# Output stages of a two-attention kernel: where chunks are scaled and split, which engine adds the biases, and the order behind the norm

## Chip, cores and metric

The kernel runs on one core of a Trainium2 chip. Its time is the device time of one execution in microseconds (us); three runs of a kernel are compared by their median. TensorE (PE) multiplies, VectorE (DVE), ScalarE (ACT) and GpSimd (Pool) work on elements, SyncE (SP) issues most of the DMA transfers. Each engine works through its own instructions in order and waits on semaphores for the others.

## What is computed

The input x has 2 sequences of 1024 tokens and 512 features. All matrices are 512 wide, in float32.

```python
x = x + attn_a(layernorm(x)) @ Wo          # 32 heads of 16, latent k and v, rotary positions
x = x + ffn(layernorm(x))                  # x @ W_eff + bias, W_eff = W.T with the LoRA products folded in
x = x + attn_b(layernorm(x)) @ w_proj + b_proj   # q, k, v from w_attn + b_attn; causal, ALiBi
x = x + ffn(layernorm(x))                  # the same ffn again
```

## The kernel before

x stays in SBUF as `x_sb`, 16 tiles of 128 tokens by 512. The work has five parts: projections for attention A (0 to 184 us), attention A (to 885), an output stage called `mid` (to 1182), attention B (to 1653) and an output stage called `fin` (to the end). Each part is one block of instructions for all engines, and the next block begins when all engines are through.

**The attentions** (`run` in `attention_plan`) go through 16 groups of 4 heads, one `step(s)` each. In a step TensorE makes the scores and the value products of group s, and ahead of them the plain scores of the next group for VectorE to take the maxima of (L353, L356). ScalarE takes exponentials (L673) and copies the sums out (L664); SP stores them to DRAM (`oa_sums`, `ob_sums`; the softmax denominators to `za_sums`, `zb_sums`). Pool splits the maxima (L279, L281), and at the end of attention B it also splits two weights into a high and a low part (`to_split`: cast L504, subtraction L506). Attention B works with three slots of memory for the operands of a group, `o_qk`, `second_qk` and `slot_qk`; the last group uses `o_qk`.

**`Output`** brings the sums back by chunks of 512 tokens, of which there are 4 (NC). `load_denominators` and `reciprocals` (L1298) turn the denominators of two chunks around through DRAM; `load(c)` fetches the sums of a chunk (1 MB, L1308) and its reciprocals, broadcast to all rows (4 transfers, L1318); `scale(c)` multiplies the two on VectorE, four instructions of 128x512 (L1324). The sums have two buffers, the broadcast reciprocals one, so `load(c)` waits for `scale(c - 1)` before its last four transfers. In both attentions chunk 0 is loaded in the last step (`s == NG - 1`) and scaled when VectorE is through with the maxima.

**`output_and_ffn`** is both output stages. For step k it makes, in TensorE's order (`order`, written out by hand, also gives each product its PSUM bank, the 8 banks in turn): two tiles of the output product `o` of chunk k, the transposes of the normalised chunk k - 1 (`f_turns`), the other two tiles of `o`, in `mid` also the transposes for the q, k, v projections of chunk k - 2 (`q_turns`), the ffn product `f` of chunk k - 1 (4 tiles), and in `mid` the projections `qk` (8 tiles) and `v` (4 tiles) of chunk k - 2. In `mid` products `o` and `f` are plain float32 (L1505); in `fin` they are made of three products of high and low parts (`split_products`, L806), for which `output_high` (ScalarE, L1576) and `output_low` (VectorE, L1655) split the scaled chunk.

VectorE's order in step k is: the low parts of the transposes (L1649), `scale(k + 1)`, the residual additions of `o` (L1620), with b_proj behind each four in `fin` (L1625), the norm of chunk k (L837 to L850, with Pool's power L855 between), at k = 0 the reciprocals of chunks 2 and 3, `output_low(k + 1)`, in `mid` at k = 0 the split of w_attn (L1682), then the residual of `f` (k - 1) with the ffn bias (L1625) and in `mid` the norm for q. In the last chunk of `mid` TensorE puts maxima of attention B's first groups between its products, in three PSUM banks that both share (`wait_left`).

```python
for k in range(STEPS):
    if fast and 0 <= k - 1 < NC:
        turned_low(f_xnt, k - 1, f_turns[k - 1])
    if k + 1 < NC:
        output.scale(dve, k + 1)
    ...
    if k < NC:
        residual("o", k, out_bias, o_added)
```

Of the kernel before, what the change touches and what calls it, by code (L numbers as in the profile page):

```python
# [1 line left out]

# [12 lines left out]
P = 128  # L15
# [143 lines left out]
def attention_plan(early, nc, ctx, tag, causal, consts, ready, ps_m, rows_of_maxima):  # L159
# [285 lines left out]
    def run(scale, q_d, k_d, v_d, o_d, z_d, alibi_d, ones_d, more, output, late, to_split):  # L445

        with ExitStack() as run_ctx:
# [30 lines left out]
            def _(pool):  # L478
# [24 lines left out]
                for n, (whole, high, low_part) in enumerate(to_split):  # L503
# [3 lines left out]
                                       ALU.subtract).then_inc(w_split, 1)  # L507
                if to_split:
# [3 lines left out]
            def _(sp):  # L512
# [15 lines left out]
                def step(s, j, ahead=True, loads=True):  # L528
# [4 lines left out]
                    if s == NG - 2:  # L533
# [721 lines left out]
class Output:  # L1255
# [6 lines left out]
    def __init__(self, nc, ctx, tag, o_d, z_d, rz_d, o_memory=None, sums=None):  # L1262
# [18 lines left out]
        self.o_scaled = sem("o_scaled")  # L1281

# [45 lines left out]
def output_and_ffn(nc, env, tag, output, w_out, out_bias, nxt, w_eff, early, first=None, second=None):  # L1328
# [28 lines left out]
    with ExitStack() as ctx:  # L1357
# [6 lines left out]
        banks = Banks(nc, ctx, tag, order, early, PT + TPC if nxt else 0)  # L1364
# [4 lines left out]
        if fast:  # L1369

            halves = [slice(n * KC * CHUNK, (n + 1) * KC * CHUNK) for n in range(2)]
            o_parts = [env["first_qk"][:, half].rearrange("p (k t) -> p k t", k=KC) for half in halves]
            o_high_ready = sem("o_high_ready")
            o_split = sem("o_split")
            f_xnt = [env["second_qk"][:, half].rearrange("p (k t) -> p k t", k=KC) for half in halves]
# [3 lines left out]
        added = sem("added")  # L1379
# [20 lines left out]
        o_added, f_added, n = {}, {}, 0  # L1400
        for k in range(STEPS):
            if k < NC and out_bias is not None:
                n += TPC
                o_added[k] = n
            if 0 <= k - 1 < NC:
                n += TPC
                f_added[k - 1] = n

# [7 lines left out]
        def _(sp):  # L1416
            output.load(sp, 1)
# [8 lines left out]
            for k in range(STEPS):  # L1426
# [5 lines left out]
                if not nxt and 0 <= c < NC:  # L1432
                    for t in range(TPC):
                        sp.wait_ge(added, f_added[c] - TPC + t + 1)
# [37 lines left out]
        def _(pe):  # L1472
# [36 lines left out]
            for k in range(STEPS):  # L1509
                def products(tiles):  # L1510
                    natural("o", k, o_parts if fast else [output.o_sb[:, k % 2]], w_out, tiles=tiles)

                if k < NC:

                    pe.wait_ge(o_split if fast else output.o_scaled, KC * (k + 1))
                    products(range(TPC // 2))
                if 0 <= k - 1 < NC:
                    f_norm.transposes(pe, banks, k - 1, f_turns[k - 1], ident)
                if k < NC:
                    products(range(TPC // 2, TPC))  # L1520
# [28 lines left out]
        def _(act):  # L1549
# [20 lines left out]
            def output_high(k):  # L1570
                for kc in range(KC):
                    act.wait_ge(output.o_scaled, KC * k + kc + 1)
                    if k and kc == 0:

                        banks.wait_full(act, ("o", k - 1, TPC - 1))
                    act.activation(o_parts[0][:, kc, :], output.o_sb[:, k % 2, kc, :],  # L1576
                                   ACT.Copy).then_inc(o_high_ready, 1)

            if fast:
                output_high(0)  # L1580
# [288 lines left out]
```

## Time and profile before

| what | value |
|---|---|
| median of 3 runs | 1784.81 us (1781.09 to 1786.96) |
| profiled execution, its own time | 1787.05 us |
| its span, first to last instruction | 1785.2 us |
| mean granted TensorE clock | 0.967 |
| TensorE busy | 1646.3 us, 92% |
| VectorE busy | 1393.8 us, 78% |
| ScalarE busy | 971.8 us, 54% |
| Pool busy | 138.6 us, 8% |

The profile is of one execution. Busy time counts instructions that compute; issuing a transfer or waiting does not count. The granted clock is a share of TensorE's full 2.4 GHz. A row of the timeline gives start, length, engine, line of the kernel, operation and tiles; "x4" is four instructions merged in one row, and in brackets stands how long the engine was idle before it and what released it. "PE" matmuls in `mid` and `fin` have 128 x 512 results; a float32 tile of 512 columns shows as 8 records of L1505, a split tile as 12 of L806.

### The profile page before, as it was taken

How to read it: one execution, taken by the hardware profiler on the slowest of the kernel's cores; microseconds unless marked ns; L12 is line 12 of the kernel's file. 1: busy time of each engine (PE TensorE's matmuls, PEld its weight loads, DVE VectorE, ACT ScalarE, POOL GpSimd, SP SyncE). 2: the span in 40 equal slices, each digit the busy share in tenths (PEclk: the TensorE clock that was granted, in tenths of full speed). 3: DMA queues.
4: the chain of work that ended last, by engine and by line, in shares of the span. 5: the costliest groups of instructions: out<-in, count | busy, mean ns of one | idle time of the engine just before them, and what ended most of it. 6: DMA issues, size and time to landing. Idle time of an engine off the chain costs nothing. (4 is left out here: it accounts for less than half of the span.)

```text
span 1785.2 us, 32918 instructions
## 1 busy us (share of the span) xinstructions
PE 1646.3 (92%) x13040; PEld 849.3 (48%) x13040; DVE 1393.8 (78%) x3007; ACT 971.8 (54%) x1103; POOL 138.6 (8%) x216
## 2 busy tenths in 40 slices
PE   6898999999999999999879999899999999999598
PEld 3554333333333333333335777555454545454476
DVE  3766799999999999999366364568888888885486
ACT  3432277777777777777711112126666666667110
POOL 3332200000000000000000011010000000003000
PEclk9999699999999999999999999989999999999799
DMA  7766334333333332330260433663636363632311
GB/s 217 226 165 193 81 56 85 63 62 64 60 63 65 55 55 56 56 55 12 86 196 1 141 116 104 202 155 57 118 73 103 65 109 60 108 61 63 103 71 71
DMA packets 116801, 167.58 MB, mean 94 GB/s; under 512 B 20772, under 2 KB 58036, under 8 KB 116532
## 3 DMA queue, kind: packets, MB, share of 16 engines
q1 hardware_dynamic: 115176, 160.99, 39.1%
q0 software_dynamic: 1472, 4.49, 1.3%
q8 instruction: 103, 1.69, 0.4%
q14 instruction: 50, 0.41, 0.1%
HBM read 100.41 MB, written 64.50 MB: 92 GB/s over the span
## 5 line engine op out<-in xcount | busy, mean ns | idle before, releaser
L356 DVE TENSOR_REDUCE mxp<-ps_m 128x1 f32<-128x512 f32 x1280 | 799.3, 684 | 69.3 <-PE ps_m L322 63.6
L673 ACT ACTIVATE a_p<-a_ps_s 128x1024 f32<-128x1024 f32 x512 | 522.2, 1025 | 149.8 <-PE a_ps_s L594 138.4
L673 ACT ACTIVATE b_p<-b_ps_s 128x1024 f32<-128x1024 f32 (+1 forms) x320 | 294.7, 938 | 157.9 <-PE b_ps_s L594 154.6
L353 DVE CUSTOM_DVE_ANT_0 ps_m<-ps_m,b_masks 128x128 f32<-128x128 f32 (+3 forms) x512 | 240.1, 517 | 45.1 <-PE ps_m L322 40.9
L322 PE MATMUL ps_m<-slot_qk 62*128 62x512 f32 (+3 forms) x624 | 230.7, 451 | 12.4 <-DVE mxp L356 9.0
L322 PE MATMUL ps_m<-a_slot_qk 62*128 62x512 f32 x640 | 238.1, 450 | 0.8
L594 PE MATMUL a_ps_s<-a_slot_qk 64*128 64x512 f32 x640 | 232.2, 443 | 1.3
L618 PE MATMUL a_ps_o<-a_p,a_slot_v 128*32 128x256 f32 x2560 | 205.6, 390 | 10.0 <-ACT a_p L673 5.4
L594 PEld LDWEIGHTS a_ps_s<-a_slot_qk 64*128 64x128 f32 x640 | 96.2, 185 | 128.8 <-issue 122.7
L594 PE MATMUL a_ps_s<-slot_qk 64*128 64x512 f32 x384 | 136.3, 455 | 0.6
L618 PE MATMUL a_ps_o<-a_p,slot_memory 128*32 128x256 f32 x1536 | 124.3, 393 | 7.4 <-ACT a_p L673 3.3
L322 PEld LDWEIGHTS ps_m<-slot_qk 62*128 62x128 f32 x624 | 101.3, 191 | 39.8 <-DVE mxp L356 27.7
L618 PEld LDWEIGHTS a_ps_o<-a_p,a_slot_v 128*32 128x32 f32 x2560 | 54.9, 108 | 115.1 <-ACT a_p L673 101.5
L574 PE MATMUL b_ps_s<-b_masks 64*128 64x64 bf16 x1024 | 102.1, 197 | 3.0 <-PEq L1357 2.6
L322 PE MATMUL ps_m<-o_qk 62*128 62x512 f32 (+3 forms) x288 | 94.6, 408 | 9.7 <-DVE mid_q_xnt L1649 6.2
L322 PEld LDWEIGHTS ps_m<-a_slot_qk 62*128 62x128 f32 x640 | 99.1, 184 | 9.3 <-DVE mxp L356 8.0
L279 POOL CAST cparts<-negm 128x16 fp32r<-128x16 f32 x64 | 12.6, 197 | 1139.8 <-DVE negm L362 1139.8
L594 PEld LDWEIGHTS a_ps_s<-slot_qk 64*128 64x128 f32 x384 | 56.4, 188 | 78.7 <-issue 74.9
L322 PE MATMUL ps_m<-second_qk 62*128 62x512 f32 (+2 forms) x240 | 87.1, 415 | 3.2 <-DVE mxp L356 1.9
L594 PE MATMUL b_ps_s<-o_qk 64*128 64x512 f32 (+3 forms) x288 | 85.4, 426 | 0.0
L574 PEld LDWEIGHTS b_ps_s<-b_masks 64*128 64x128 bf16 x1024 | 54.8, 96 | 59.0 <-issue 45.1
L1562 ACT ACTIVATE slot_memory<-mid_ps,b_qk 128x512 fp32r<-128x512 f32 x23 | 15.8, 689 | 109.0 <-PE mid_ps L806 92.8
(205 smaller groups left out, 2343.7 us busy)
## 6 DMA issues: line engine op xcount, KB each, us to landing
va_groups<-w_o SPq DMA_DIRECT2D x16, 512.0 KB, 3.7
ka_parts<-pa_parts SPq DMA_DIRECT2D x16, 512.0 KB, 3.8
qa_parts<-pa_parts SPq DMA_DIRECT2D x32, 256.0 KB, 3.7
kb_parts<-slot_memory SPq DMA_DIRECT2D x16, 512.0 KB, 4.1
qb_parts<-slot_memory SPq DMA_DIRECT2D x32, 256.0 KB, 3.8
vb_groups<-w_proj SPq DMA_DIRECT2D x16, 512.0 KB, 3.4
a_slot_qk<-qa_parts SPq DMA_DIRECT2D x60, 128.0 KB, 4.1
a_slot_qk<-ka_parts SPq DMA_DIRECT2D x48, 128.0 KB, 6.3
```

Source lines behind the costliest of these rows:

```text
L279: pool.tensor_copy(cparts[:, :, 0, :], split(negm[:, :])).then_inc(high_ready, 1)
L322: pe.matmul(ps_m[:, bank_of(g, i), 0:keys], q, k, start=True, stop=True).then_inc(piece_ready, 1)
L353: dve.tensor_tensor_reduce(from_, from_, mask_of_query[:, CHUNK - keys:], 1.0, LOWEST, ALU.add, ALU.max, accum_out=to).then_inc(piece_take ...
L356: dve.tensor_reduce(to, from_, AX.X, ALU.max).then_inc(piece_taken, 1)
L574: pe.matmul(to[:, half * ROW_TILE:(half + 1) * ROW_TILE], mask[tile, half, :], half_ident[tile, :], start=(half == 0), stop=False, skip_gr ...
L594: mm = pe.matmul(to[:, at:at + n], k, q, start=not diagonal, stop=True, skip_group_check=diagonal)
L618: mm = pe.matmul(ps_o[VW * h:VW * (h + 1), off:off + n], slots[j].v[:, kt, VW * h:VW * (h + 1)], p_sb[:, (2 * u + h // 2) % NP, h % 2, at: ...
L673: act.activation(p_sb[:, (2 * u + pair) % NP, :, off:CHUNK], ps_s[:, 2 * pair:2 * pair + 2, off:CHUNK], ACT.Exp, scale=scale).then_inc(exp ...
L1562: act.activation(parts[:, n % PARTS, 0, :], banks.out(("qk", c, i)), ACT.Identity, bias=bias_of(i)).then_inc(high_ready, 1)
```

## The change

- **Chunks 0 and 1 in the attentions' last groups.** Denominators, reciprocals and loads of the first batch move one step earlier (`NG - 3`, `NG - 2`), and `load(1)` is new in the last step. At the end of VectorE's list stand `scale(0)` and `scale(1)`. In attention B both are split there as well, high parts by Pool (`high_pool`) and low parts by VectorE (`low`), into two buffers of parts in `second_qk` and `slot_qk`, which groups 13 and 14 have left. In `fin` the transposed chunk moves to `o_qk`.
- **Biases by Pool.** b_proj is added to x by Pool in attention B, one tile behind each part of the maxima (`to_add`), before the output stage. The ffn bias is added by Pool behind the norm of the tile it belongs to (`biased`), before the residual of `f`. VectorE's L1625 is gone.
- **Scaling behind the norm.** `scale(k + 1)` and, in `fin`, its split come after the norm of chunk k, for chunks 2 and 3 only. `reciprocals(1)` comes first in the stage. The split of w_attn moves from k = 0 to k = 1.
- **Transposes behind 3 products**: three tiles of `o`, the transposes, the fourth tile, in TensorE's order and in the banks. VectorE takes the residuals of the first three tiles, the low parts of the transposes, then the fourth residual.
- In `mid` the last 16 tasks (with the last q transposes) use the five own banks, before it was the last 12.

```diff
@@ run of attention_plan
+                adds = iter(to_add)
                 for g in range(1, NG):
                     for qh in range(2):
                         parts_of_maxima(g, qh)
+                        for tile, bias in itertools.islice(adds, 1):
+                            pool.tensor_tensor(tile, tile, bias, ALU.add)
...
+                if output.split:
+                    for c in range(2):
+                        pool.wait_ge(pv_done, (NG - 2 + c) * NU)
+                        output.high_pool(pool, c)
...
-                    if s == NG - 2:
+                    if s == NG - 3:
                         for qh in range(2):
                             sp.wait_ge(out_stored[qh], output.STORES * s)
                         output.load_denominators(sp, 0)
-                    if s == NG - 1:
+                    if s == NG - 2:
                         output.store_reciprocals(sp, 0)
                         output.load(sp, 0)
+                    if s == NG - 1:
+                        output.load(sp, 1)
...
-                    if s == NG - 2:
+                    if s == NG - 3:
                         output.reciprocals(dve, 0)
-                output.scale(dve, 0)
+                for c in range(2):
+                    output.scale(dve, c)
+                    if output.split:
+                        output.low(dve, c)
@@ class Output
+    def high_pool(self, pool, c):
+        for kc in range(KC):
+            pool.wait_ge(self.o_scaled, KC * c + kc + 1)
+            pool.tensor_copy(self.parts[c % 2][0][:, kc, :], self.o_sb[:, c % 2, kc, :]).then_inc(self.high_ready, 1)
...
+    def low(self, dve, c):
+        for kc in range(KC):
+            dve.wait_ge(self.high_ready, KC * c + kc + 1)
+            dve.tensor_tensor(self.parts[c % 2][1][:, kc, :], self.o_sb[:, c % 2, kc, :],
+                              self.parts[c % 2][0][:, kc, :].bitcast(F32), ALU.subtract).then_inc(self.split_ready, 1)
@@ output_and_ffn
-            order += [("o", k, t) for t in range(TPC // 2)]
+            order += [("o", k, t) for t in range(TPC - 1)]
         if 0 <= k - 1 < NC:
             order += f_turns[k - 1]
         if k < NC:
-            order += [("o", k, t) for t in range(TPC // 2, TPC)]
+            order += [("o", k, TPC - 1)]
...
-        banks = Banks(nc, ctx, tag, order, early, PT + TPC if nxt else 0)
+        banks = Banks(nc, ctx, tag, order, early, KC + PT + TPC if nxt else 0)
...
-            output.load(sp, 1)
...
-                if fast and k + 1 < NC:
-                    output_high(k + 1)
+                if fast and 2 <= k + 1 < NC:
+
+                    banks.wait_full(act, ("o", k - 1, TPC - 1))
+                    output.high_act(act, k + 1)
...
                     f_norm.gpsimd(pool, k)
+                    for t in range(TPC):
+                        tile = x_sb[:, k * TPC + t, :]
+                        pool.wait_ge(f_norm.xn_ready, k * TPC + t + 1)
+                        pool.tensor_tensor(tile, tile, w["bias"][:, :], ALU.add).then_inc(biased, 1)
...
+            output.reciprocals(dve, 1)
             for k in range(STEPS):
-                if fast and 0 <= k - 1 < NC:
-                    turned_low(f_xnt, k - 1, f_turns[k - 1])
-                if k + 1 < NC:
-                    output.scale(dve, k + 1)
                 if nxt and k == 2:
                     dve.wait_ge(ones_set, 1)
                 if k < NC:
-                    residual("o", k, out_bias, o_added)
+                    residual("o", k, range(TPC - 1))
+                if fast and 0 <= k - 1 < NC:
+                    turned_low(f_xnt, k - 1, f_turns[k - 1])
+                if k < NC:
+                    residual("o", k, [TPC - 1])
                 if nxt and 0 <= k - 2 < NC:
                     turned_low(q_xnt, k - 2, q_turns[k - 2])
                 if k < NC:
                     f_norm.vector(dve, k, k, k and (lambda: banks.wait_full(dve, f_turns[k - 1][-1])))
...
-                if nxt and k == 0:
+                if 2 <= k + 1 < NC:
+                    output.scale(dve, k + 1)
+                    if fast:
+                        output.low(dve, k + 1)
+                c = k - 1
+                if 0 <= c < NC:
+                    residual("f", c)
+                    if nxt:
+                        q_norm.vector(dve, c, c, c and (lambda: banks.wait_full(dve, q_turns[c - 1][-1])))
+                if nxt and k == 1:
                     for kc in range(KC):
                         dve.wait_ge(w_high_ready, kc + 1)
```

## Rows read from the trace of the kernel before

**Rows 1.** Windows by stage: length; busy (instructions) PE, PEld, DVE, ACT, POOL; clock, DMA, GB/s
```profile
884.90:1182.00 297.10, 277.30 (x1012) 175.88 (x1012) 162.00 (x319) 44.07 (x69) 17.62 (x15) 0.97 0.44 132
1182.00:1653.00 471.00, 444.89 (x4876) 236.01 (x4876) 395.84 (x1266) 312.21 (x352) 33.64 (x74) 0.98 0.46 84
1653.00:1785.20 132.20, 102.74 (x448) 83.44 (x448) 86.95 (x162) 17.04 (x32) 4.05 (x4) 0.89 0.24 83
```

**Rows 2.** Waits, 1650 to 1786 us: us in total, times, longest
```profile
PE fin_ps L806 <- DVE o_qk L1655: 22.1, 4, 13.3
...
PE fin_ps L806 <- DVE second_qk L1649: 2.3, 1, 2.3
```

**Rows 3.** Timeline, first output stage: start, length, instruction, [idle before <- releaser]
```profile
914.67 5.02 DVE L1682 TENSOR_TENSOR mid_w_qkv<-slot_memory,mid_w_qkv 128x1536 fp32r<-128x1536 f32 x3
...
926.89 2.50 DVE L1324 TENSOR_TENSOR o_memory<-o_memory,out_a_rzt 128x512 f32<-128x512 f32 x4 [5.52 <-DMA out_a_rzt<-za_reciprocals]
...
930.04 5.49 PE L1505 MATMUL mid_ps<-w_eff,ffn_memory 128*128 128x512 f32 x8 [8.39 <-DVE x_sb L1620]
...
935.37 10.46 PE L1505 MATMUL ps_m<-w_eff,ffn_memory 128*128 128x512 f32 x24
```

**Rows 4.** Timeline, end of the first output stage
```profile
1127.88 0.69 DVE L1641 TENSOR_TENSOR w_proj<-ps_m,b_v 128x512 f32<-128x512 f32 x1 [9.47 <-DMA vb_groups<-w_proj]
...
1130.00 2.47 DVE L1649 TENSOR_TENSOR mid_q_xnt<-mid_ps,mid_q_xnt 128x512 fp32r<-128x512 f32 x4
...
1131.04 0.47 PE L322 MATMUL ps_m<-o_qk 62*128 62x128 f32 x2 [6.24 <-DVE mid_q_xnt L1649]
```

**Rows 5.** Chain of waits in order of time, one chunk of the last stage
```profile
1705.04 2.47 DVE fin_f_stats L837 x4
...
1709.11 1.92 DVE fin_f_xn L850 x4
...
1711.04 2.42 DVE o_qk L1655 x4
```

**Rows 6.** Timeline of Pool and VectorE, projections at the start
```profile
62.17 2.70 POOL L1174 TENSOR_TENSOR o_memory<-o_memory,pa_cos 128x512 f32<-128x512 f32 x2
...
62.24 3.83 DVE L850 TENSOR_SCALAR ffn_memory<-x_sb,pa_mv,pa_rstd 128x512 f32<-128x512 f32 x4 [1.12 <-POOL pa_rstd L855]
...
72.58 0.69 DVE L1204 TENSOR_TENSOR w_q<-pa_ps,pa_sin 128x512 f32<-128x512 f32 x1 [1.81 <-PE pa_ps L1040]
...
73.12 1.27 POOL L1174 TENSOR_TENSOR o_memory<-w_proj,pa_cos 128x512 f32<-128x512 f32 x1
...
73.31 1.63 DVE L1208 TENSOR_TENSOR w_q<-o_memory,w_q 128x512 f32<-128x512 f32 x1
```

**Rows 7.** End of attention B: Pool's groups of 1629.5 to 1652.4 us, then timeline
```profile
L506 POOL TENSOR_TENSOR w_proj_low<-w_proj,w_proj_high 128x2048 fp32r<-128x2048 f32 x1 | 4.6, 4554 | 0.1
...
L504 POOL CAST w_proj_high<-w_proj 128x2048 fp32r<-128x2048 f32 x1 | 1.9, 1891 | 0.0
...
1635.90 2.54 SPq L1318 DMA_DIRECT2D out_b_rzt<-zb_reciprocals  x4
...
1646.56 2.50 DVE L1324 TENSOR_TENSOR out_b_o_t<-out_b_o_t,out_b_rzt 128x512 f32<-128x512 f32 x4 [15.69 <-DMA out_b_rzt<-zb_reciprocals]
...
1653.56 1.83 SPq L525 DMA_DIRECT2D ob_sums<-out_b_sums  x4
```

**Rows 8.** Windows of products in the last stage, and its last transposes from the timeline
```profile
1659.00:1664.40 5.40, 5.38 (x13) 4.28 (x14) 0.00 (x0) 0.00 (x0) 0.00 (x0) 0.53 0.73 230
1664.40:1672.60 8.20, 8.20 (x36) 6.41 (x35) 4.30 (x7) 0.00 (x0) 0.00 (x0) 1.00 0.18 56
1766.60:1771.10 4.50, 4.46 (x13) 3.59 (x14) 1.69 (x3) 0.00 (x0) 0.00 (x0) 0.63 0.22 84
...
1762.47 1.91 PE L865 MATMUL fin_ps<-ident,fin_f_xn 128*128 128x128 f32 x16
```

**Rows 9.** Timeline, VectorE's last instructions
```profile
1780.06 2.49 DVE L1625 TENSOR_TENSOR x_sb<-x_sb,b_ffn 128x512 f32<-128x512 f32 x4
```

More of the change, by code:

```diff
@@ L443, in attention_plan, with run @@
     early.tensor, early.vector, early.banks = early_tensor, early_vector, ps_m
-    def run(scale, q_d, k_d, v_d, o_d, z_d, alibi_d, ones_d, more, output, late, to_split):
+    def run(scale, q_d, k_d, v_d, o_d, z_d, alibi_d, ones_d, more, output, late, to_split, to_add):
         with ExitStack() as run_ctx:
@@ L1281, in __init__ @@
         self.o_scaled = sem("o_scaled")
+        self.split = parts_memory is not None
+        if self.split:
+            self.parts = [[m[:, n * KC * CHUNK:(n + 1) * KC * CHUNK].rearrange("p (k t) -> p k t", k=KC)
+                           for n in range(2)] for m in parts_memory]
+            self.high_ready = sem("o_high_ready")
+            self.split_ready = sem("o_split")
     STORES = 16 * (GH + 1)
@@ L1510, in products @@
                 def products(tiles):
-                    natural("o", k, o_parts if fast else [output.o_sb[:, k % 2]], w_out, tiles=tiles)
+                    natural("o", k, output.parts[k % 2] if fast else [output.o_sb[:, k % 2]], w_out, tiles=tiles)
                 if k < NC:
-                    pe.wait_ge(o_split if fast else output.o_scaled, KC * (k + 1))
-                    products(range(TPC // 2))
+                    pe.wait_ge(output.split_ready if fast else output.o_scaled, KC * (k + 1))
+                    products(range(TPC - 1))
                 if 0 <= k - 1 < NC:
@@ L1569, in _ @@
                     act.activation(w_qkv[0][:, kc, :], w_whole[kc], ACT.Copy).then_inc(w_high_ready, 1)
[L1570 to L1580, printed above, removed]
             for k in range(STEPS):
@@ L1615, in _, with residual @@
         def _(dve):
-            def residual(kind, c, bias, counts):
-                for t in range(TPC):
+            def residual(kind, c, tiles=range(TPC)):
+                for t in tiles:
                     task, tile = (kind, c, t), x_sb[:, c * TPC + t, :]
                     banks.wait_full(dve, task)
+                    if kind == "f":
+                        dve.wait_ge(biased, c * TPC + t + 1)
                     dve.tensor_tensor(tile, banks.out(task), tile, ALU.add).then_inc(banks.drain(task), 1)
-                for t in range(TPC):
-                    task, tile = (kind, c, t), x_sb[:, c * TPC + t, :]
-                    banks.wait_drained(dve, task)
-                    if bias is not None:
-                        dve.tensor_tensor(tile, tile, bias[:, :], ALU.add).then_inc(added, 1)
-                if bias is not None:
-                    dve.wait_ge(added, counts[c])
+                for t in tiles:
+                    banks.wait_drained(dve, (kind, c, t))
             def low(c, i):
@@ L1683, in _ @@
                                           ALU.subtract).then_inc(w_split, 1)
-                c = k - 1
-                if 0 <= c < NC:
-                    residual("f", c, w["bias"], f_added)
-                    if nxt:
-                        q_norm.vector(dve, c, c, c and (lambda: banks.wait_full(dve, q_turns[c - 1][-1])))
                 c = k - 2
@@ L1804, in build @@
                         [(env["w"]["proj"][:, :, :], env["w_proj"].rearrange("(k p) n -> p k n", p=P))],
-                        [(env["w"][name], *split[name]) for name in ("proj", "eff")])
-            output_and_ffn(nc, env, "fin", output, split["proj"], env["w"]["bproj"], False, split["eff"], early_b)
+                        [(env["w"][name], *split[name]) for name in ("proj", "eff")],
+                        [(env["x_sb"][:, n, :], env["w"]["bproj"][:, :]) for n in range(TILES)])
+            output_and_ffn(nc, env, "fin", output, split["proj"], False, split["eff"], early_b)
 def in_parts(x):
```

47 lines of the change are left out of this document (16 added, 31 removed).

## Prediction

> **What bounds the kernel now.** I read first the windows by stage [rows 1]. TensorE is busy 277.3 of 297.1 us in the first output stage and 102.7 of 132.2 us in the last one, where its granted clock is 0.89 against 0.97 and 0.98. In the attentions it is above 94%. So idle TensorE is to be had in the two output stages and hardly elsewhere: 19.8 and 29.5 us, and some more where the clock is low.
>
> Then the waits, and what ended each. In the last stage four waits of 22.1 us together (longest 13.3) are for the low parts of the attention output [rows 2]. In the first output stage TensorE stood 8.4 us for a residual addition of VectorE [rows 3] and 6.2 us for VectorE's low parts of the last q transposes [rows 4]. The timeline says what was late behind the 8.4 us [rows 3]: VectorE sat 5.52 us in `scale(2)`, which waits for the broadcast reciprocals; the residuals that free the PSUM banks are queued behind it. After the wait a product tile takes 5.49 us, where three later ones take 10.46. For the 6.2 us [rows 4]: VectorE stood 9.47 us because the stores of v came late. In SP's order they stand behind the stores of this chunk's k and q and the loads of the next attention's first group, so this end hangs on when VectorE gives SP its first piece, and four bias additions (2.49 us, as in [rows 9]) lie ahead of that. In the last stage the chain of waits runs through VectorE and Pool from one chunk to the next [rows 5].
>
> **First output stage, step by step.** The profiled execution took 1787.05 us, its span is 1785.2, the median of the runs is 1784.81; I sum against the span and carry the difference over.
> - Chunk 1 is loaded and scaled inside attention A, whose VectorE is idle after its last maxima. o(0) runs as now, and o(1) follows with no wait.
> - Three product tiles of o(1) (10.5 us by the three of f in [rows 3]) go ahead of the transposes, so these wait for no norm. f(0) finds its banks drained, since the residuals are no longer behind `scale(2)`: the 8.4 us wait goes, and 2.0 us of low clock behind it (5.49 against 10.46 / 3 = 3.49).
> - The split of w_attn (three of its four instructions took 5.02 us [rows 3], so 6.7 of VectorE) moves to k = 1, behind it Pool's memset of 128x2048 (I take 1.9, as the Pool cast of that size in [rows 7]) and then the residuals of o(2), on which the first q transposes wait: by my schedule about 0.5 us lost; f(0)'s 14 us and three tiles of o(2) cover the rest. Sum to the first q product: 8.4 + 2.0 - 0.5 = 9.9.
> - The end: the last f tile sets VectorE; without the biases its first piece comes 2.5 us earlier, SP's row of DMAs with it, and the 6.2 us wait shrinks by that. The q transposes of the last chunk now use the five banks that are not shared with the maxima, so the first maxima needn't wait for them: 0.7 us (of the 1.0 from 1130.00 to 1131.04, [rows 4]). Stage: 9.9 + 2.5 + 0.7 = 13.1 us gained.
>
> **The price: Pool's bias additions beside VectorE.** Four additions of 128x512 a chunk now start as each normalised tile is ready, while VectorE still normalises the next. Rows of the first stage show what the two do to each other [rows 6]: with two Pool tensor_tensors beside them, four normalisations took 3.83 us instead of 1.92 [rows 5], 0.95 us for each Pool instruction; a VectorE tensor_tensor with both inputs in SBUF took 1.63 instead of 0.69, also 0.94 more; one that reads PSUM and SBUF took 0.69, untouched. The engines take turns. So two additions fall between the normalisations (+1.9) and the other two between the four multiplications of `scale`, where one follows (+1.9); residuals are not touched. Bounds: 0 (VectorE keeps ahead), and 4 x 1.27 = 5.1 if each holds VectorE for its length. I take 3.8, the measured delay. The Trainium skill, page SBUF — State Buffer, section "SBUF: two separate sides", says the pair shared by VectorE and GpSimd is an exclusive lock, and the loser "fully blocks", also for a VectorE operation with two SBUF inputs. The trace agrees in kind; by its letter the sum would be the upper bound, 5.1 a chunk. In the first output stage 3.8 us a chunk stay hidden: o(1) covers chunk 0, f(0) of 14 us covers chunk 1; without that cover each would cost its 3.8.
>
> **End of attention B.** `scale(0)`, with two SBUF inputs, now starts at about 1630.4, beside Pool's two casts and two subtractions of the weights (1.89 and 4.55 us each, [rows 7]). Taking turns, its four instructions end at about 1643.5 instead of 1632.8. SP issues the reciprocals of chunk 1 only then. Now they and the 1 MB of outputs land 10.7 us after the first issue (1635.90 to 1646.56); without the 1 MB I take 8.5, so 1652. Scale, Pool's casts and the low parts by turns: 5.6, to 1657.6. SP's last DMA of the block used to set its end, 1655.4 [rows 7]; now VectorE does, and the stage begins at 1658.0. Bounds: 1655.9 (no turns), 1660.5 (10.7 us again). SP also holds the store of group 15's first half behind this wait, without cost, as the second half's store comes later still.
>
> **Last output stage.** A product tile takes 2.73 us, the first one after a pause 5.4 at a granted clock of 0.53, about the lower level of 1.2 GHz [rows 8]; the transposes of a chunk take 1.8 (1.91 to the end of the last [rows 8]). From the stage's start: o(0) 5.4 + 8.2 = 13.6. Chunk 1 is split already: three tiles, 21.8; transposes, which wait 0.4 for the fourth normalised tile, 24.0; fourth tile 26.7. From there VectorE's way to o(2): residual 0.6, norm to its last tile 6.0 (1705.04 to 1711.03), low parts 2.4 [rows 5], scale 2.4 (four instructions of the same size, 2.50 with the last one's end [rows 3]), and 3.8 for Pool: 15.3 with rounding. f(0), 11.0 us, covers it except 4.3, and after such a pause the clock is low again (1.8 more for the tile after a wait of 2.3 us [rows 2, 8], 2.6 after a longer one; I take 2.3). o(2) starts at 42.0; three tiles 52.5, transposes 54.3, fourth 57.0. The same once more: o(3) starts at 72.3, its fourth tile ends at 87.3. Chunk 3 has no successor: f(2) to 98.3, transposes 100.1, f(3) 111.1. Residual 0.7. The last additions of b_ffn (2.49, [rows 9]) are gone, also those of b_proj (2.5 a chunk, done by Pool in attention B); from VectorE's last instruction (1782.55) to the end of the span 2.7 as now. Total 114.5; 1658.0 + 114.5 = 1772.5, which is 12.7 us before 1785.2.
>
> **Attentions.** The reciprocals of batch 0 (1.8 us of VectorE) move one group earlier. In A there is a like place now. In B they fall where VectorE is busy nearly all of a group (395.8 of 471.0 us over the whole attention, its last group idle [rows 1]), and delay maxima on which TensorE waits: up to 1.8. The 16 additions of b_proj run beside VectorE instructions that read PSUM and at most one SBUF operand, the untouched kind: 0, at most 16 x 0.94 = 15. The moved DMAs (two denominators, two reciprocals, one load of five) cost SP some 5 us in a group of about 29 (471.0 / 16), well before the next load it owes. I take 1.5 us lost in all.
>
> **Sum.** 13.1 + 12.7 - 1.5 = 24.3 us: span 1760.9, profiled 1762.8, and against the median of 1784.81, 1760.5 us.
>
> **Rivals.**
> - No price for Pool: VectorE keeps ahead and nothing takes turns. The stage begins at 1655.9; both stalls shrink from 4.3 to 0.5 us and cost no clock: 2.1 + 2 x (3.8 + 2.3) + 0.4 = 14.7 more. 1745.8 us. For it: Pool's first addition can only start after the second normalisation is under way. Against: the turns in [rows 6].
> - Dearer: each addition blocks for its length, the reciprocals are late (+2.5), the stalls grow by 1.3 each, the first stage gets a stall and low clock (3), the attentions lose 2 more: 10 us back, 1770. For it: at the end of attention B VectorE, Pool and SP now work one behind the other. Against: the 0.94 us of [rows 6]. It is also where the Trainium skill's rule of the exclusive lock (page and section as above) leads.
> - The maxima of attention B do collide with b_proj's additions: 15 us back, 1775. The untouched instruction in [rows 6] speaks against it.
> - Slower: the pauses of 4.3 us leave TensorE's clock at its low level through the rest of the last stage. Then 20 tiles from o(2) on take 5.4 instead of 2.73 and the kernel ends 29 us later than now, at 1813 (24.3 gained, 53 lost). It decides from 9 tiles at the low level. Against: after the pause ahead of the stage's first product and the one of 2.3 us the clock was full, or all but, one tile later [rows 8].
> - The change doesn't do what it says: chunk 1 ready only after the stage's start. That needs the block's end past VectorE, which it waits for; then the start is late instead, as priced.
>
> **Chances.** As summed 0.52; no price 0.19; dearer 0.18; collision in B 0.04; lost to within 0.3% (5.4 us, what a measurement here can tell from no change) by several of these 0.03; slower 0.04. So faster 0.93, same 0.03, slower 0.04. The range goes from just below the no-price case to just above the dearer one: 1744 to 1772.
>
> **What would show it.** No wait ahead of the first f product and first q product some 10 us earlier; normalisation rows of 3.8 us a chunk with Pool additions of 1.3 to 1.7 between; in attention B's end `scale(0)` stretched over some 13 us and the last stage starting near 1658; there two TensorE waits of about 4 us before o(2) and o(3), none of 13; no addition after the last residual. Wrong if the normalisations take 1.9 or if the waits before o(2) and o(3) pass 7 us.

## The result, and the profile after

The changed kernel takes 1765.03 us (median of 4 runs, 1764.1 to 1765.98) against 1784.47 us for the kernel before (4 runs, 1781.09 to 1786.96): ratio 0.9892, 95% interval 0.9875 to 0.991. The forecast was 1760.5 us in a range of 1744 to 1772. The profiled execution took 1764.37 us with a span of 1762.2 (before 1787.05 and 1785.2).

I cut both traces at the same four places: first o product of the first output stage (`mid`), first score product of attention B, last value product of B, first o product of the last stage (`fin`). Each part is the difference of two rows of TensorE's timeline:

| part | before | after | gained | forecast |
|---|---|---|---|---|
| start to `mid` | 887.93 | 886.86 | 1.07 | 0 |
| `mid` | 295.99 | 282.48 | 13.51 | 13.1 |
| attention B to its last product | 468.38 | 469.21 | -0.83 | -1.5 |
| from there to `fin` | 6.72 | 7.21 | -0.49 | 1.0 |
| `fin` to the end of the span | 126.18 | 116.44 | 9.74 | 11.7 |

The windows by stage after answer to [rows 1]; the last three lie behind TensorE's restarts at 1687.75 (5.5 and 7.25 us) and 1719.40 (5.5 us), ahead of o(2) and o(3):
```profile
886.80:1169.30 282.50, 274.43 (x1012) 175.02 (x1012) 160.58 (x299) 44.27 (x68) 40.79 (x31) 0.98 0.44 133
1169.30:1638.60 469.30, 445.05 (x4876) 235.83 (x4876) 410.84 (x1270) 311.88 (x351) 58.06 (x94) 0.98 0.48 87
1645.70:1762.20 116.50, 103.09 (x448) 83.75 (x448) 73.55 (x118) 13.19 (x24) 27.56 (x20) 0.92 0.21 75
...
1687.70:1693.20 5.50, 5.45 (x13) 4.31 (x14) 2.38 (x4) 0.00 (x0) 0.00 (x0) 0.50 0.77 259
1687.75:1695.00 7.25, 7.25 (x20) 5.75 (x21) 3.02 (x5) 0.00 (x0) 0.00 (x0) 0.59 0.71 245
1719.40:1724.90 5.50, 5.50 (x14) 4.36 (x15) 2.35 (x5) 0.00 (x0) 0.00 (x0) 0.54 0.51 191
```
TensorE's idle time in `mid` fell from 19.8 to 8.1 us, in `fin` from 29.5 to 13.4. Its waits in `fin`, which answer to [rows 2]:
```profile
PE fin_ps L822 <- PEq L449: 7.2, 1, 7.2
PE fin_ps L822 <- DVE second_qk L1369: 4.8, 1, 4.8
PE fin_ps L822 <- DVE slot_qk L1369: 4.8, 1, 4.8
PE ps_m L881 <- DVE fin_f_xn L866: 0.3, 1, 0.3
```
In place of four waits of 22.1 us there are two of 4.8, ahead of o(2) and o(3). Behind each, TensorE ran at the lower of its two clock levels, 1.2 GHz instead of 2.4. The first 7.25 us from the first restart had a granted clock of 0.59, which is 7.25 x 0.41 = 3.0 us lost; behind the second it is 5.5 x 0.46 = 2.5 us. VectorE's way to o(2), its timeline (answers to [rows 5]):
```profile
1676.81 3.88 DVE L866 TENSOR_SCALAR fin_f_xn<-x_sb,fin_f_mv,fin_f_rstd 128x512 f32<-128x512 f32 x4 [1.13 <-POOL fin_f_rstd L871]
1680.61 4.67 DVE L1348 TENSOR_TENSOR out_b_o_t<-out_b_o_t,out_b_rzt 128x512 f32<-128x512 f32 x4
1685.21 2.48 DVE L1369 TENSOR_TENSOR second_qk<-out_b_o_t,second_qk 128x512 fp32r<-128x512 f32 x4
```
and Pool beside it:
```profile
1677.43 6.09 POOL L1627 TENSOR_TENSOR x_sb<-x_sb,b_ffn 128x512 f32<-128x512 f32 x4 [0.66 <-DVE fin_f_xn L866]
```
Pool's additions lie under the normalisation and the scaling, and both are stretched; the low parts behind them are not. Within the four scalings only two are stretched, and the first stands alone in a narrower view:
```profile
1680.61 1.78 DVE L1348 TENSOR_TENSOR out_b_o_t<-out_b_o_t,out_b_rzt 128x512 f32<-128x512 f32 x1
```
At the end of attention B (answers to [rows 7]), VectorE and then SP:
```profile
1616.64 13.87 DVE L1348 TENSOR_TENSOR out_b_o_t<-out_b_o_t,out_b_rzt 128x512 f32<-128x512 f32 x4
1631.02 3.70 DVE L1369 TENSOR_TENSOR second_qk<-out_b_o_t,second_qk 128x512 fp32r<-128x512 f32 x4 [0.50 <-POOL second_qk L1356]
1638.88 3.32 DVE L1348 TENSOR_TENSOR out_b_o_t<-out_b_o_t,out_b_rzt 128x512 f32<-128x512 f32 x4 [4.17 <-DMA out_b_rzt<-zb_reciprocals]
1642.13 3.31 DVE L1369 TENSOR_TENSOR slot_qk<-out_b_o_t,slot_qk 128x512 fp32r<-128x512 f32 x4
```
```profile
1630.60 2.55 SPq L1342 DMA_DIRECT2D out_b_rzt<-zb_reciprocals  x4
...
1639.82 1.83 SPq L536 DMA_DIRECT2D ob_sums<-out_b_sums  x4
```
`scale(0)` lasts 13.87 us beside Pool's split of the weights; SP asks for chunk 1's reciprocals when it ends; VectorE's work ends last (1642.13 + 3.31 = 1645.44), behind the issue of SP's last store. In `mid` the 8.4 us wait is gone, one of 1.9 stands ahead of the first q transposes, and the wait of 6.2 us at the end ([rows 4]) is 2.7:
```profile
PE ps_m L324 <- issue: 2.7, 1, 2.7
...
PE mid_ps L881 <- DVE x_sb L1649: 1.9, 1, 1.9
```

### The profile page after: what moved, and what is told of

It reads as the page before. It is cut to its first block and busy times, and to the rows that moved or that the text cites. A ratio compares the mean times of both kernels' runs of the same rounds, so it can differ in the third digit from the quotient of the medians.

```text
span 1762.2 us, 32974 instructions
## 1 busy us (share of the span) xinstructions
PE 1643.6 (93%) x13040; PEld 848.8 (48%) x13040; DVE 1402.5 (80%) x2959; ACT 969.0 (55%) x1095; POOL 213.8 (12%) x272
## 5 line engine op out<-in xcount | busy, mean ns | idle before, releaser
L324 PE MATMUL ps_m<-slot_qk 62*128 62x512 f32 (+3 forms) x624 | 230.9, 451 | 12.2 <-DVE mxp L358 8.9
```

The source lines that it names most:

```text
L324: pe.matmul(ps_m[:, bank_of(g, i), 0:keys], q, k, start=True, stop=True).then_inc(piece_ready, 1)
```

## The experiments

The theory was that Pool's additions of b_ffn, where they stand, cost the two waits and the clock behind them, and that Pool's split of the weights makes `fin` start late. The rival was that VectorE's chain or SP sets both anyway. All edits are against the changed kernel. The parts are by the same cuts, from each profile. Only `fin` is cut short here, at the end of its last product in a bank of `fin_ps`; three more tiles, 8.2 us in every kernel, follow it.

| kernel | `mid` | B | gap | `fin` | span | median |
|---|---|---|---|---|---|---|
| before | 295.99 | 468.38 | 6.72 | 112.15 | 1785.2 | 1784.47 |
| after | 282.48 | 469.21 | 7.21 | 105.02 | 1762.2 | 1765.03 |
| v1_pool_late | 281.39 | 470.11 | 6.59 | 91.04 | 1744.5 | 1751.65 |
| v2_split_early | 282.57 | 478.47 | 3.54 | 103.50 | 1760.9 | 1763.01 |
| v3_bias_vector | 288.15 | 472.95 | 6.99 | 93.62 | 1762.1 | 1764.98 |
| v4_two_products | 286.61 | 472.56 | 7.97 | 109.44 | 1772.5 | one run |
| v5_chunk1_in_stage | 283.90 | 472.73 | 3.53 | 113.05 | 1768.4 | one run |
| v6_both | 280.77 | 470.24 | 3.53 | 90.82 | 1740.5 | 1746.47 |
| v7_halves | 281.81 | 472.27 | 6.89 | 103.54 | 1760.7 | one run |
| v8_both_apart | 281.74 | 467.95 | 3.53 | 92.17 | 1741.5 | 1743.67 |
| v9_banks | 284.44 | 472.79 | 7.70 | 103.11 | 1765.2 | one run |
| v10_scale_first | 284.56 | 474.98 | 7.11 | 103.39 | 1765.5 | one run |
| v11_wsplit_first | 286.85 | 468.27 | 7.39 | 105.23 | 1764.9 | one run |
| v12_all | 281.40 | 469.25 | 3.53 | 91.63 | 1742.5 | 1743.18 |

The start of `mid`, behind code that is nearly the same in all, varies from 881.5 to 887.9 us; so spans of single runs are compared part by part. A part varies as well. `mid` is the same code in the changed kernel, v2 and v5: 282.5, 282.6 and 283.9 us. `fin` is the same in the changed kernel, v2, v9, v10 and v11: 105.0, 103.5, 103.1, 103.4 and 105.2 us. In `fin` the waits are the same too (4.8 us twice); what differs is how long the clock stays low behind them. A difference of 2 us in a part, seen in one profile, is therefore not resolved by the time alone.

**v1_pool_late.**
```diff
+                    pool.wait_ge(f_norm.xn_ready, (k + 1) * TPC)
+                    if 2 <= k + 1 < NC:
+                        pool.wait_ge(output.split_ready if fast else output.o_scaled, KC * (k + 2))
                     for t in range(TPC):
                         tile = x_sb[:, k * TPC + t, :]
-                        pool.wait_ge(f_norm.xn_ready, k * TPC + t + 1)
                         pool.tensor_tensor(tile, tile, w["bias"][:, :], ALU.add).then_inc(biased, 1)
```


> Pool adds b_ffn only when VectorE has normalised the chunk and scaled (in the last stage also split) the next one, so no addition lies beside a VectorE instruction with two SBUF inputs. Theory (the two engines take turns on such instructions, and that alone makes the two waits of 4.8 us): four normalisations 1.9 instead of 3.87 us, four multiplications 2.4 instead of 4.67; the two waits of TensorE fall to 0.6 us each, the low clock behind them (about 2.7 us each) goes; last stage 116.4 to about 103 us, span 1762.2 to about 1748.5, median about 1751. Rival 1 (the waits come from VectorE's chain itself, or the residuals of f now wait for the late additions): the last stage stays within 2 us of 116.4, 1763 to 1767. Rival 2 (the waits go but the clock is low anyway): two times 4.2 us, median about 1757.

VectorE's timeline of the same chunk, and then Pool's:
```profile
1672.57 1.92 DVE L866 TENSOR_SCALAR fin_f_xn<-x_sb,fin_f_mv,fin_f_rstd 128x512 f32<-128x512 f32 x4 [1.13 <-POOL fin_f_rstd L871]
1674.40 2.49 DVE L1348 TENSOR_TENSOR out_b_o_t<-out_b_o_t,out_b_rzt 128x512 f32<-128x512 f32 x4
```
```profile
1679.45 5.06 POOL L1629 TENSOR_TENSOR x_sb<-x_sb,b_ffn 128x512 f32<-128x512 f32 x4 [6.92 <-DVE second_qk L1369]
```
Waits of TensorE and the window of `fin`:
```profile
PE fin_ps L822 <- DVE second_qk L1369: 0.6, 1, 0.6
PE fin_ps L822 <- DVE slot_qk L1369: 0.6, 1, 0.6
```
```profile
1642.00:1744.50 102.50, 97.69 (x448) 79.93 (x448) 61.57 (x118) 13.02 (x24) 24.30 (x20) 0.98 0.24 85
```
Both waits are 0.6 us, the clock is 0.98, `fin` is 14.0 us shorter: 8.4 of waits, 5.5 of clock, 0.1 elsewhere. Median 1751.65 us, ratio to before 0.9825 (0.980 to 0.9849). The profiled execution was the fastest of the four (1746.69); by the medians the gain is 13.4 us. The theory holds (`fin` with its end 102.4 us, 103 expected); both rivals fell.

**v2_split_early.** Pool's split is cut by kc and done one piece behind each part of the maxima from group 9 on.
```diff
-                for n, (whole, high, low_part) in enumerate(to_split):
-                    pool.tensor_copy(high[:, :, :], whole[:, :, :]).then_inc(w_high_ready, 1)
...
+                pieces = iter([(*t, kc) for t in to_split for kc in range(KC)])
...
                         parts_of_maxima(g, qh)
+                        for whole, high, low_part, kc in itertools.islice(pieces, 1 if g >= 9 else 0):
...
+                            pool.tensor_copy(high[:, kc, :], whole[:, kc, :]).then_inc(w_high_ready, 1)
...
```


> The split of w_proj and w_eff on Pool is cut into pieces of 128x512 and moved from the end of attention B into its groups 9 to 12. Theory (the late start of the last stage comes from scale(0) of chunk 0 being stretched by Pool's casts and subtractions to 12.3 us, behind which SP's load of the reciprocals waits): scale(0) takes 2.5 us, the last VectorE instruction of the block ends about 3.7 us earlier, the gap from the last PV product to the stage's start falls from 7.2 to 3.5 us; span 1762.2 to about 1758.5, median about 1761.5. Rival (the gap is set by SP's last stores, or by the loads themselves): gap stays above 6 us, median 1764 to 1766. A loss is possible if the pieces delay Pool's small work on the maxima in groups 9 to 12: it would show as TensorE waits inside attention B.

VectorE's timeline, and windows of 5 us in group 14:
```profile
1620.54 2.48 DVE L1352 TENSOR_TENSOR out_b_o_t<-out_b_o_t,out_b_rzt 128x512 f32<-128x512 f32 x4
...
1636.56 3.33 DVE L1352 TENSOR_TENSOR out_b_o_t<-out_b_o_t,out_b_rzt 128x512 f32<-128x512 f32 x4 [9.34 <-DMA out_b_rzt<-zb_reciprocals]
```
```profile
1584.00:1589.00 5.00, 3.86 (x48) 2.16 (x48) 4.82 (x18) 2.40 (x4) 0.42 (x2) 1.00 0.07 17
1589.00:1594.00 5.00, 5.00 (x43) 2.38 (x40) 2.92 (x12) 2.54 (x3) 0.00 (x0) 0.54 0.47 122
1594.00:1599.00 5.00, 5.00 (x37) 3.22 (x35) 2.88 (x11) 1.80 (x3) 0.00 (x0) 0.50 0.68 252
```
The end went as the theory says: `scale(0)` 2.48 us, gap 3.54. But B took 9.3 us more. Its windows show two stretches at half clock, this one and one from about 1238, behind a wait of 1.72 us for the shift rows. v6_both, with the same split, has neither (470.24 us), so the split is not their cause. Median 1763.01, ratio 0.9875 (0.9854 to 0.9895): its gain alone is not resolved from the changed kernel.

**v3_bias_vector.** Pool's four additions go; VectorE adds b_ffn behind the residuals of f, and SP's store waits for that.
```diff
                 for t in tiles:
                     banks.wait_drained(dve, (kind, c, t))
+                    if kind == "f":
...
+                        dve.tensor_tensor(tile, tile, w["bias"][:, :], ALU.add).then_inc(biased, 1)
```


> b_ffn is added by VectorE again, behind the residual of each f product, in both output stages; b_proj stays with Pool in attention B. Theory (the price of the moved additions is their turns with VectorE): normalisations 1.9, multiplications 2.4 us, both waits of 4.8 us fall to 0.6 and their low clock goes (about -14), but four additions (2.5 us) are back behind the last residual of each stage, so +2.5 at the end and +2.5 at the end of the first output stage: span about 1753, median about 1756. Rival (the moved additions are worth what they were moved for): VectorE becomes the bound again, its 2.5 us a chunk bring the waits back, median 1765 or more.

`fin` to its last product is 11.4 us shorter, and the four additions are back behind it:
```profile
1756.93 2.49 DVE L1648 TENSOR_TENSOR x_sb<-x_sb,b_ffn 128x512 f32<-128x512 f32 x4
```
The two waits are 0.6 us again, so in `fin` the theory of the turns holds here too. But a wait that I had not counted, 2.26 us ahead of f(3), stands for low parts behind VectorE's additions:
```profile
1745.05 0.47 PE L822 MATMUL fin_ps<-w_eff_high,o_qk 128*128 128x512 f32 x1 [2.26 <-DVE o_qk L1672]
```
With the four additions at the end, `fin` as a whole is 8.8 us shorter. What I had more wrong is `mid`, 5.7 us longer where I expected 2.5:
```profile
PE ps_m L324 <- DVE w_proj L1664: 6.0, 1, 6.0
...
PE mid_ps L881 <- DVE x_sb L1643: 3.0, 1, 3.0
```
against 2.7 and 1.9 in the changed kernel. The median, 1764.98 us, is that of the changed kernel, as the rival had it (1765 or more), though not by the rival's waits. In the two profiles b_ffn on Pool gains 5.7 us in `mid` and loses 8.8 in `fin`; what evens this out is B, 3.7 us longer here, with a stretch at half clock that the changed kernel's profile lacks (see the last section).

**v4_two_products.** `TPC - 1` back to `TPC // 2` in the order, the banks, TensorE's and VectorE's lists.

> Transposes of the normalised chunk again behind two of the four o products, the rest as changed. Theory (the fourth normalised tile is ready just as the third product ends): the transposes of f wait for the normalisation by a product's time less what is hidden, in the last stage 2.3 us for chunk 0 and nothing for chunks 1 and 2, whose transposes come long after the norm; in the first output stage the residuals on which f's banks hang come earlier in VectorE's row. Together +2 to +5 us, span 1764 to 1767. Rival (the order of products is indifferent): span within 1 us of 1762.2.

`mid` is 4.1 and `fin` 4.4 us longer, more than I expected. Two of the waits for the norm of chunk 0 in `fin`, of which I had counted 2.3 us together and no clock:
```profile
1672.22 0.33 PE L881 MATMUL ps_m<-ident,fin_f_xn 128*128 128x128 f32 x1 [1.08 <-DVE fin_f_xn L866]
1673.63 1.33 PE L881 MATMUL ps_m<-ident,fin_f_xn 128*128 128x128 f32 x5 [1.08 <-DVE fin_f_xn L866]
```
In this profile the order is worth 8.5 us. The waits make up about half: TensorE waits 1.8 us more in `fin` and 1.9 more in `mid`. The clock is the other half: summed over slices of 1 us, (1 - granted clock) x length is 10.9 us instead of 8.7 in `fin` and 6.8 instead of 4.7 in `mid`. A new low stretch stands right behind the second of the two waits shown.

**v5_chunk1_in_stage.** Chunk 1 of B is loaded, scaled and split (high parts by ScalarE) ahead of the loop of `fin`.
```diff
-                    for c in range(2):
+                    for c in range(1):
                         pool.wait_ge(pv_done, (NG - 2 + c) * NU)
                         output.high_pool(pool, c)
...
+            if fast:
+                output.scale(dve, 1)
+                output.low(dve, 1)
             output.reciprocals(dve, 1)
```


> Chunk 1 of attention B is loaded, scaled and split in the last output stage instead of in the attention's last group, the rest as changed. Theory (the late start, 7.2 us behind the last product of the attention, is the price of doing chunk 1 there; in the stage its 8.5 us of load lie beside o(0) of 14 us): the gap falls to about 3.6 us, chunk 1 is split about 15 us into the stage, TensorE waits up to 2 us ahead of o(1); last stage to its last product 105 to 108 us; sum within 3 us of the changed kernel. Rival (doing chunk 1 early is what removed the old waits): a wait of over 5 us ahead of o(1), sum 5 us or more worse.

```profile
1661.36 0.50 PE L822 MATMUL fin_ps<-w_proj_high,slot_qk 128*128 128x512 f32 x1 [3.94 <-DVE slot_qk L1369]
```
The gap is 3.53 us as expected, but the reciprocals landed 12.5 us after the stage's start, not 8.5, and o(1) waited 3.94 us. `fin` is 8.0 us longer: chunk 1 in attention B is worth 8.0 - 3.7 = 4.3 us. That lies between the theory (within 3) and the rival (5 or more); the wait, 3.94 us, does too.

**v7_halves.** Each addition of 128x512 as two of 128x256.

> Each of Pool's additions of b_ffn (128x512) is cut into two of 128x256: the same work in twice as many instructions. If each turn costs VectorE the rest of one Pool instruction, halving them lowers the price: normalisations below 3.87 us, nearer to 2.9, multiplications below 4.67. If what counts is the bandwidth of shared work (both engines slowed in proportion), the two stay at 3.9 and 4.7 us. Last stage 112 to 116.5 us by the one, 116 to 118 by the other.

```profile
1676.95 2.76 DVE L866 TENSOR_SCALAR fin_f_xn<-x_sb,fin_f_mv,fin_f_rstd 128x512 f32<-128x512 f32 x4 [1.13 <-POOL fin_f_rstd L871]
1679.63 4.66 DVE L1348 TENSOR_TENSOR out_b_o_t<-out_b_o_t,out_b_rzt 128x512 f32<-128x512 f32 x4
1684.21 3.54 DVE L1369 TENSOR_TENSOR second_qk<-out_b_o_t,second_qk 128x512 fp32r<-128x512 f32 x4
```
Neither theory as written. The three together take 10.96 us, 11.03 in the changed kernel, and 6.90 in v1_pool_late: the price is 4.1 us either way. Halves take half the turn each (normalisation 2.76 instead of 3.88), but there are twice as many: all four scalings are stretched (4.66 in sum, as before), and the rest lands on the low parts (3.54 instead of 2.48). `fin`, 103.54 us, is no shorter than with whole additions (103.1 to 105.2).

**v10_scale_first.** In `mid` alone, `scale(k + 1)` stands ahead of the residuals of o(k) again.

> In the first output stage alone, VectorE scales chunk k + 1 ahead of the residuals of o(k) again; chunk 1 is still scaled in attention A, all else as changed. Theory (the old wait of 8.4 us came from the residuals being queued behind scale(2), which waits for the broadcast reciprocals; moving the scaling behind the norm took it away, not the early chunk 1): TensorE waits again ahead of the first f product, 5 to 9 us, with a low clock behind it; stage 282.5 to 289 to 294 us. Rival (early chunk 1, with its earlier loads, is what took it away): scale(2) finds its reciprocals landed and the stage stays within 2 us of 282.5.

```profile
910.44 2.72 DVE L1348 TENSOR_TENSOR o_memory<-o_memory,out_a_rzt 128x512 f32<-128x512 f32 x4 [1.99 <-DMA out_a_rzt<-za_reciprocals]
```
My theory fell: `mid` is 2.1 us longer (1.2 of it a longer wait ahead of the first q transposes, 3.1 instead of 1.9) and no wait stands ahead of f(0). `scale(2)` begins 26.4 us into the stage (910.44 - 884.03), 39.0 before (926.89 - 887.93). The reciprocals come 12.5 us earlier, and with them in time the place of the scaling matters little. The reverse, the new order with late reciprocals, was not run.

**v9_banks.** `KC + PT + TPC` back to `PT + TPC`.

> The transposes of the last q chunk use all eight PSUM banks again instead of the five that are not shared with the first maxima of attention B. Theory: the wait of TensorE behind the last q transposes' drain is 0.7 us longer, stage 283.2 instead of 282.5. Rival (the end of the stage hangs on the loads of the first group alone): no change, 282.5 within 0.5.

The wait at the end of `mid` is 3.65 us for the low parts of the transposes instead of 2.68: 1.0, where I had 0.7. The stage is 2.0 longer; the other 1.0 is clock, 5.7 us lost in the stage instead of 4.7 by the same sum over slices. This half is scatter: v5, with `mid` unchanged, has the longer low stretch at the same place and takes 283.9 us.

**v11_wsplit_first.** `if nxt and k == 1` back to `k == 0` for the split of w_attn, ahead of the scaling.

> VectorE splits w_attn at k = 0, behind the norm of chunk 0, instead of at k = 1. Theory (the 1.94 us wait of TensorE ahead of the first q transposes comes from the split and Pool's memset behind it, both ahead of the residuals of o(2)): the wait falls to 0.7 us or less and the stage is 1 to 2 us shorter, 280.5 to 281.5, if f(0) finds its banks. Rival (the split at k = 0 delays the residuals of o(1) and so f(0), which it was moved for): a wait of 2 to 5 us ahead of the first f product, stage 284 or more.

```profile
920.60 4.97 PE L1537 MATMUL mid_ps<-w_eff,ffn_memory 128*128 128x512 f32 x7 [2.78 <-DVE x_sb L1649]
```
The rival held: the wait ahead of the q transposes goes, one of 2.78 us ahead of f(0) comes, and the stage is 4.4 us longer.

**v6_both, v8_both_apart, v12_all**: v1 and v2 together; with the two reciprocals of group 13 apart; with v11's edit as well.

> Late additions of b_ffn and early split of the weights together. Theory (independent places): last stage to its last product 91 us as with the late additions alone, gap ahead of it 3.5 us as with the early split alone, first output stage 281.4; attention B 469 to 478 us, depending on how often a short wait of TensorE in it is followed by a low clock. Span 1736 to 1748, likeliest 1741, median about 1744. Rival (the early split itself costs attention B some 9 us, as it seemed in its own run): B again 478 us and median about 1750, no better than the late additions alone.

> As the run with both, and the two reciprocals that VectorE computes back to back behind the maxima of group 13 in attention B stand apart: one in the middle of that group's maxima, one at the end. Theory (1.8 us of VectorE in one piece let TensorE wait 0.97 us for its maxima there, and after that wait the clock was low for about 10 us in three of five kernels, some 4 to 5 us each time): the wait falls to 0.3 us or less, no low clock near group 14, B at most 470 us; median 2 to 4 us below the run with both. Rival (the wait is not the cause of the low clock, or z's load comes too late for the middle of the group, so that VectorE stands there): a low stretch at the same place, or a new wait of TensorE inside group 13; the same time or more.

> The run with both and the reciprocals apart, and the split of w_attn at k = 0 as well. Theory: first output stage 280 instead of 281.7, the rest as there: median 1742, 1739 to 1745. Rival: the split at k = 0 costs more than it gives back, median 1745 to 1750.

v6 is v1's `fin` and v2's gap, as expected: median 1746.47 us, ratio 0.979 (0.977 to 0.981). v8: 1743.67, 0.9781 (0.9756 to 0.9807); its wait did not fall to 0.3 us but moved, 0.9 us in group 13. v12: 1743.18, 0.978 (0.9763 to 0.9798). The three are not told apart by time; each beats both kernels. In v12, where Pool's additions no longer slow VectorE, the early split of w_attn costs nothing, but it gains less than the 1.7 us I expected over v8 (281.40 against 281.74).

## Why the prediction was right

- **`mid`, 13.1 forecast, 13.5 measured.** Up to the first q product 9.9 us were gained (976.23 - 887.93 = 88.3 before, 965.29 - 886.86 = 78.4 after), as forecast, and 3.6 at the end, 3.2 forecast. The sum is right and its terms less so. The wait of 8.4 us went, but I gave one cause, the residuals standing behind `scale(2)`. v10_scale_first shows that the new order was not needed: with the old order back, reciprocals that land 12.5 us earlier keep the wait away. Whether the order alone would have done it too is open. The change held both, so the term came out by luck as much as by reading. The earlier landing may be due to `reciprocals(1)` standing first or to `load(1)` having left the stage; this was not tried apart, but SP's rows speak for the first. It stores the reciprocals right behind VectorE's, 26.0 us into the stage before and 4.4 after (a row of before, then one of after):
```profile
913.97 1.14 SPq L1303 DMA_DIRECT2D za_reciprocals<-out_a_z  x2
...
891.23 0.99 SPq L1327 DMA_DIRECT2D za_reciprocals<-out_a_z  x2
```
  The q transposes wait 1.94 us, not 0.5, for residuals of o(2) that stand behind Pool's memset, as VectorE's timeline says:
```profile
949.08 1.89 DVE L1649 TENSOR_TENSOR x_sb<-mid_ps,x_sb 128x512 f32<-128x512 f32 x3 [1.90 <-POOL w_proj L1621]
```
  What makes up for it lies ahead of f(0), where o(0), the first transposes and o(1) take 2.1 us less, a gain that I had put at nothing; behind f(0) some 0.6 us are lost again.
- **The price of Pool's additions** was the term to get right, and its kind and size hold: 4 x 0.95 = 3.8 us a chunk forecast, 4.1 measured (11.03 - 6.90). The term was small by 0.3, in `scale` (4.67 against 2.49): two normalisations lost 0.98 us each (3.88 - 1.92), as forecast, but two scalings 1.09 each ((4.67 - 2.49) / 2), where I had taken 0.95 for all. One scaling takes 1.78 us beside Pool and 0.68 in v1_pool_late, while beside the residuals, with one input in PSUM, Pool's additions stay at 1.27 us each (5.06 for four). Pool is held up by the turns too: beside the SBUF-only instructions its four take 6.09 us. The Trainium skill, page SBUF — State Buffer, section "SBUF: two separate sides", calls the shared pair an exclusive lock whose loser is fully blocked; the runs agree in kind, but in size four additions of 5.06 us cost VectorE 4.1, not 5.1.
- **The two waits**: 4.8 us instead of 4.3, by that 0.3 and rounding; low clock 3.0 and 2.5 instead of 2.3 each. v1_pool_late shows the chain from cause to time: additions moved, waits and low clock gone, 14.0 us. The rival "no price" put the two waits and their clock at 2 x 6.1 = 12.2. The clock's share is not fixed: in v2, v9 and v10 the same two waits of 4.8 us cost 1.5 to 1.7 us of clock each, and `fin` is 1.5 to 1.9 us shorter for it.
- **The late start**: 7.2 us behind the last value product against 5.7 forecast. `scale(0)` ended 13.9 us after its start, 13.1 forecast; the reciprocals landed 8.3 us after their first issue (8.5 forecast); the mis-sized term is scale and split of chunk 1, 6.6 us instead of 5.6, because Pool's casts stretch both. v2_split_early shows the cause. The gap it leaves, 3.5 us, is the least in any kernel here, and `mid` too begins 3.5 us behind attention A in all of them.
- **Attentions**: 1.5 us forecast, 0.8 measured. No wait of TensorE in B's profile is put down to Pool's additions of b_proj, as forecast. But the moved reciprocals left a wait that I had priced at nothing more than its length (below).
- **The sum**: the span came out 1.3 us above the 1760.9 forecast. That it came so near is partly luck: the two terms of `fin` and its late start fell short by 3.5 us, and 1.1 of that was made good by a `mid` that began earlier, which is within that start's scatter, 0.7 by B and 0.4 by `mid`. The other 3.2 us between 1760.5 and 1765.0 are the step from one profiled execution to the median: before, the profiled execution lay 2.2 us above the median (1787.05, 1784.81), after, 0.7 below it (1764.37, 1765.03), and its ends took 2.2 us instead of 1.9.

The changed kernel's largest remaining fault is where it adds b_ffn: v3_bias_vector gives the same median with the additions back on VectorE, and v1_pool_late 13.4 us less with them later on Pool.

## What to carry to other kernels

In this kernel Pool's additions were free beside VectorE's residuals, which read PSUM; next to instructions with SBUF inputs alone they cost VectorE 4.1 us for 5.06 us of their own, some four fifths, whole or in halves. Put such work behind the last such instruction of the chain that TensorE waits for: the same additions, behind the scaling and the low parts, gave 14.0 us in `fin` and 13.4 by the medians. And when a wait disappears, test which of the moved things removed it: here an earlier DMA was enough without the new order.

## What the runs showed of the hardware

A wait of TensorE of under 1 us can cost several. Moving two reciprocals to the end of group 13 made TensorE wait 0.95 to 0.98 us in group 14, in eleven of the kernels above. In seven of them the granted clock then stood at about half for some 10 us (0.54 and 0.50 in the rows of v2_split_early), in four it stayed at 1.00, as in the changed kernel:
```profile
1584.00:1589.00 5.00, 3.86 (x51) 2.38 (x43) 4.82 (x19) 2.36 (x4) 0.42 (x2) 1.00 0.09 21
1589.00:1594.00 5.00, 4.80 (x65) 2.65 (x64) 4.25 (x20) 3.67 (x5) 0.00 (x0) 1.00 0.47 137
```
The first window, with the wait in it, is the same in both: 3.86 us busy of 5. Attention B took 469.5 us on average where the clock stayed up there (four kernels, 468.3 to 470.2) and 472.7 where this was the only low stretch behind its start (five, 472.3 to 473.0): 3.2 us. That is too little for the stretch, as the start differs too. In every kernel, before included, B begins with 13 to 17 us at half clock, around or behind TensorE's pause of 2.6 us between the blocks (a row of after, then one of before):
```profile
1169.00:1185.00 16.00, 15.59 (x112) 9.31 (x114) 9.75 (x35) 7.30 (x9) 8.96 (x12) 0.50 0.69 103
1183.00:1199.50 16.50, 15.51 (x112) 9.24 (x112) 9.74 (x35) 7.23 (x8) 7.97 (x11) 0.50 0.71 111
```
This costs 6.8 us of clock in the five and in v11_wsplit_first (468.3 us), 7.9 to 8.1 in the other three whose clock stayed up. Like with like, the stretch in group 14 costs 472.7 - 468.3 = 4.4 us. The start is the longest low stretch of B in every kernel, and the change does not touch it. Other short waits in B do not decide it either: TensorE waits 0.7 to 1.9 us for the shift rows near 1240 us in twelve of the thirteen kernels from the changed one on, and the clock fell behind that in two of them only (v2, 1.72 us, and v10, 1.94), not in v12 (1.94). With the reciprocals apart (v8, v12) that wait is gone, one of 0.9 us stands in the middle of group 13, and the clock stayed up both times. Two executions don't show that this is a cure, nor did the times. What decides between the two outcomes stays open.
